# Second attention block: turning x un-normalised, with centred weights, a bias through a diagonal of deviations, and the variance from ScalarE's squares

## The reference

```
def layer_norm(x, gamma, beta):
    mu = jnp.mean(x, axis=-1, keepdims=True)
    var = jnp.mean(jnp.square(x - mu), axis=-1, keepdims=True)
    return (x - mu) * jax.lax.rsqrt(var + LN_EPS) * gamma + beta
q = (decoder_seq @ Wq.T + bq).reshape(B, T_dec, N_HEADS, D_HEAD)
kv = jnp.einsum('bthd,bthe->bhde', k, v)
att = jnp.einsum('bqhd,bhde->bqhe', q, kv) * scale
return layer_norm(att.reshape(B, T_dec, D_MODEL) + decoder_seq, ln_gamma, ln_beta)
...
x = x + jnp.tanh(g_xattn[1]) * _L1_xattn_ref(ctx_1024, _layernorm(x, axis=-1), ...)
x = x + jnp.tanh(g_ffn[1]) * _L1_ffn_ref(_layernorm(x, axis=-1), ...)
```

## Time and profile before

| | us |
|---|---|
| median of 3 runs | 739.65 (737.48 to 742.19) |
| the profiled execution | 736.21 |
| its span, first to last instruction | 734.3 |
| of that: from x back in SBUF (433.07) to the last router norm (484.38) | 51.3 |

### The profile page before, as it was taken

How to read it: one execution, slowest core, us unless ns; L and a number is a source line. 1 busy time by engine, 2 the same in 40 slices (tenths; PEclk the granted TensorE clock), 3 DMA queues, 4 the chain that set the end, 5 groups by cost and what they waited for, 6 DMA issues and landing times.

```text
span 734.3 us, 21433 instructions
## 1 busy us (share of the span) xinstructions
PE 657.8 (90%) x7365; PEld 572.6 (78%) x7366; DVE 482.6 (66%) x1218; ACT 457.4 (62%) x1113; POOL 305.6 (42%) x222
## 2 busy tenths in 40 slices
PE   4777899979988999999999969973999999999993
PEld 4423466758877999988999959862999999999992
DVE  4788678864768866666664468986697545545451
ACT  2465788735568887867766516550898666666651
POOL 1100235434724655554555333331256455554532
PEclk9866699999999999999999998855999999999997
DMA  8980101215559547799876489838564454544451
GB/s 273 371 295 8 29 2 32 85 37 166 145 196 358 85 81 184 187 200 260 215 168 111 65 239 415 289 114 184 122 125 72 73 80 72 85 75 76 70 59 21
DMA packets 114934, 105.08 MB, mean 143 GB/s; under 512 B 53611, under 2 KB 100725, under 8 KB 114246
## 3 DMA queue, kind: packets, MB, share of 16 engines
q1 hardware_dynamic: 99910, 83.93, 38.1%
q0 software_dynamic: 14976, 20.58, 18.6%
HBM read 64.84 MB, written 28.23 MB: 127 GB/s over the span
## 4 chain that ended last, share of the span: by engine, by line
PE 71%; DVE 13%; DMA 4%; ACT 4%; issue 3%; POOL 2%; SPq 1%; POOLq 0%; DVEq 0%; ACTq 0%
PE bank L1217 9%; PE bank L1219 9%; PE bank L1218 9%; PE bank L1230 9%; PE bank L1232 9%; PE bank L1231 9%; PE bank L971 2%; PE bank L972 1%; PE bank L973 1%; DVE ln_stats L2063 1%; DMA x_arena<-token_rows,gather_now 1%; DVE weights L1708 1%; POOL weights L820 1%; PE bank L1112 1%; PE bank L1129 1%
## 5 line engine op out<-in xcount | busy, mean ns | idle before, releaser
L1526 ACT ACTIVATE work<-bank,b_cols 128x128 f32<-128x128 f32 x624 | 178.5, 384 | 135.2 <-PE bank L1219 133.0
L1217 PE MATMUL bank<-x_arena,weights 128*128 128x128 f16 x1248 | 215.3, 220 | 1.3 <-DVE x_arena L1955 1.3
L1218 PE MATMUL bank<-x_arena,weights 128*128 128x128 f16 x1248 | 215.3, 220 | 0.0
L1219 PE MATMUL bank<-x_arena,weights 128*128 128x128 f16 x1248 | 215.3, 220 | 0.0
L1970 DVE TENSOR_TENSOR work<-work 128x512 f16<-128x512 f32 x156 | 101.0, 689 | 113.7 <-ACT work L1534 113.7
L1230 PE MATMUL bank<-weights,work 128*128 x624 | 170.2, 273 | 1.3 <-issue 1.3
L1232 PE MATMUL bank<-weights,work 128*128 x624 | 170.1, 273 | 0.0
L1231 PE MATMUL bank<-weights,work 128*128 x624 | 170.1, 273 | 0.0
L826 POOL DMA_INDIRECT x_arena<-token_rows,gather_now x78 | 81.7, 1047 | 141.8 <-DVE gather_now L1964 105.9
L1217 PEld LDWEIGHTS bank<-x_arena,weights 128*128 x1248 | 122.9, 98 | 2.6 <-DVE x_arena L1955 1.8
L1218 PEld LDWEIGHTS bank<-x_arena,weights 128*128 x1248 | 122.9, 98 | 0.8
(11 more groups left out here) (227 smaller groups left out, 1188.8 us busy)
## 6 DMA issues: line engine op xcount, KB each, us to landing
weights<-in_L_ffn_W SPq DMA_DIRECT2D x76, 256.0 KB, 7.1
raw<-in_L_ffn_W SPq DMA_DIRECT2D x44, 256.0 KB, 4.0
split_dram<-row_arena SPq DMA_DIRECT2D x12, 512.0 KB, 5.5
weights<-split_dram SPq DMA_DIRECT2D x3, 2048.0 KB, 15.9
odd_sum<-padding_row SPq DMA_DIRECT2D x1, 2176.0 KB, 11.5
token_rows<-row_arena SPq DMA_DIRECT2D x1, 2072.0 KB, 10.0
x_arena<-in_x SPq DMA_DIRECT2D x4, 512.0 KB, 6.3
weights<-in_L_ffn_sW SPq DMA_DIRECT2D x8, 256.0 KB, 7.3
```

The lines of the kernel that those rows point to most:

```text
L1217: nc.tensor.matmul(o, w1_at[f][c][0].block(), hi, start=c == 0, stop=False)
L1218: nc.tensor.matmul(o, w1_at[f][c][0].block(), lo, start=False, stop=False)
L1219: m = nc.tensor.matmul(o, w1_at[f][c][1].block(), hi, start=False, stop=c == DC - 1)
L1526: m = nc.scalar.activation(hid[:, k, f * P:f * P + P], h_ps[k][half][:, g * P:g * P + P], ACT.Gelu, bias=b1_cols[n][:, f, bass.ds(e, 1)], ...
```

## The change

x is no longer normalised ahead of the second attention. PE transposes x itself, as soon as the two sums are added. Wq is centred over its inputs, and the folded matrix and the bias over their outputs, so that the means of x and of the result vanish. What the normalisation would have scaled is put on the bias: it is multiplied by the standard deviation of each token, as a matmul with a diagonal matrix (`diag`) that ACT makes from the identity. The second normalisation cancels the common factor; its epsilon is scaled to match (`mid_shift[:, norm1(1, b)]`). The variance of the result is the mean of squares that ACT sums (`accum_out`), so DVE takes no moments of it. The lists of calls on all engines and `MID_NORMS` change with it; `shift1` is left for the router's norms only, so waits on `shift_ready` count to B.

```diff
+diag = work[:, 0:1024].rearrange("p (k t r) -> p k t r", k=2, t=TB)
+squares_out = work[:, 1024:1024 + TB * D].rearrange("p (t d) -> p t d", t=TB)
+kvm_mean = places[:, 0, 0:B * DC].rearrange("p (b c) -> p b c", b=B)
+plus_half = places[:, 1, TT - TB:TT]
+kvb_mean, wq_mean = places[:, 1, 0:B], places[:, 1, B:B + DC]
...
-MID_NORMS = [0, 1, 2, 3, 4, 5, 8, 6, 9, 7, 10, 11]
+MID_NORMS = [0, 1, 2, 4, 8, 3, 5, 9, 6, 10, 7, 11]
...
         pool.wait_ge(var1_ready, after)
-        nc.gpsimd.tensor_tensor(mid_rstd[:, i, :], mid_rstd[:, i, :], minus_half[:, :], ALU.pow).then_inc(rstd1_ready, 1)
+        if i < B:
+            nc.gpsimd.tensor_tensor(mid_shift[:, i, :], mid_rstd[:, i, :], plus_half, ALU.pow).then_inc(rstd1_ready, 1)
+        else:
+            nc.gpsimd.tensor_tensor(mid_rstd[:, i, :], mid_rstd[:, i, :], minus_half[:, :], ALU.pow).then_inc(rstd1_ready, 1)
+    nc.gpsimd.memset(plus_half, 0.5).then_inc(consts_ready, 1)
+    pool.wait_ge(consts_ready, 6)
     for count, i in enumerate(MID_NORMS):
         mid_roots(i, count + 1)
         if count == 9:
             router_rows_low(0)
-    pool.wait_ge(shift_ready, 2 * B)
+    pool.wait_ge(shift_ready, B)
...
     def turned1(b, h):
-        pe.wait_ge(ln_done, 2 * B + half_no(b, h))
+        pe.wait_ge(ln_done, 2 * B + 2 * b + 2)
         if b:
             pe.wait_ge(xlnT_ready, half_no(b - 1, h))
         for c in range(DC):
             for t in range(2):
-                m = nc.tensor.transpose(half_ps(h)[:, c, t * P:t * P + P], normed(8 + b)[:, 2 * h + t, c * P:c * P + P], ident)
+                m = nc.tensor.transpose(half_ps(h)[:, c, t * P:t * P + P], x_sb[:, TB * b + 2 * h + t, c * P:c * P + P], ident)
         m.then_inc(tp_done, 1)
     def attention1(b, h):
+        if h == 0 and b < 2:
+            pe.wait_ge(act_setup, 6 if b == 0 else 10)
+        elif h == 0:
+            pe.wait_ge(attended, TB * (b - 1))
         pe.wait_ge(xlnT_ready, half_no(b, h))
         for t in range(2 * h, 2 * h + 2):
-            i = TB * b + t
             for c in range(DC):
-                m = nc.tensor.matmul(attended_ps(i), xlnT[:, b % 2, c, t * P:t * P + P], kvm[:, b, c, :], start=False, stop=t % 2 == 1 and c == DC - 1)
-            m.then_inc(proj_done, 1)
+                nc.tensor.matmul(attended_ps(TB * b + t), xlnT[:, b % 2, c, t * P:t * P + P], kvm[:, b, c, :], start=t % 2 + c == 0, stop=False)
+    def bias1(b):
+        pe.wait_ge(act_setup, (8, 11, 12, 13)[b])
+        for t in range(TB):
+            nc.tensor.matmul(attended_ps(TB * b + t), diag[:, b % 2, t, :], kvb[:, b, :], start=False, stop=t % 2 == 1).then_inc(proj_done, 1)
...
-    bias1(0)
+    for h in range(2):
+        turned1(0, h)
     for b in range(B):
-        for h in range(2):
-            turned1(b, h)
-        if b == 0:
+        if b == 1:
             folded(2)
             folded_bias(2)
-        else:
-            bias1(b)
+        if b < B - 1:
+            for h in range(2):
+                turned1(b + 1, h)
         for h in range(2):
             attention1(b, h)
+        bias1(b)
...
-        act.wait_ge(pe_setup, 10 + first)
-        for i in range(2):
-            m = nc.scalar.activation(kvm[:, first + i, :, :].rearrange("p c e -> p (c e)"), fold_ps[i][:, :], ACT.Copy)
+        act.wait_ge(dve_setup, 10 + first)
+        for b in range(first, first + 2):
+            for c in range(DC):
+                m = nc.scalar.activation(kvm[:, b, c, :], fold_ps[b - first][:, c * D:c * D + D], ACT.Identity, bias=kvm_mean[:, b, c:c + 1])
         m.then_inc(act_setup, 1)
-        act.wait_ge(pe_setup, 11 + first)
-        nc.scalar.activation(kvb[:, first:first + 2, :].rearrange("p b d -> p (b d)"), kv_ps[first // 2][:, :], ACT.Copy).then_inc(act_setup, 1)
+        act.wait_ge(dve_setup, 11 + first)
+        for b in range(first, first + 2):
+            m = nc.scalar.activation(kvb[:, b, :], kv_ps[first // 2][:, b % 2 * D:b % 2 * D + D], ACT.Identity, bias=kvb_mean[:, b:b + 1])
+        m.then_inc(act_setup, 1)
...
-    def norm_x(b, h):
+    def deviations(b):
+        act.wait_ge(rstd1_ready, rstd1_count(0, b))
         if b >= 2:
-            act.wait_ge(tp_done, B + half_no(b - 2, h))
-        normalise1(x_sb[:, TB * b:TB * b + TB, :], normed(8 + b), norm1(0, b), b + 1, h).then_inc(ln_done, 1)
+            act.wait_ge(proj_done, TT + TB * (b - 1))
+        for t in range(TB):
+            m = nc.scalar.activation(diag[:, b % 2, t, :], ident, ACT.Copy, scale=mid_shift[:, b, t:t + 1])
+        m.then_inc(act_setup, 1)
+    def attended_squares(b, h):
+        act.wait_ge(proj_done, TT + TB * b + 2 * h + 2)
+        if b:
+            act.wait_ge(squared, half_no(b - 1, h))
+        for t in range(2 * h, 2 * h + 2):
+            m = nc.scalar.activation(squares_out[:, t, :], attended_ps(TB * b + t), ACT.Square, accum_out=mid_mv[:, norm1(1, b), t, 1:2])
+        m.then_inc(squared, 1)
...
-    halves(norm_x, 0)
     halves(read_out1, 0)
+    deviations(0)
+    halves(read_out1, 1)
     folded_out(2)
-    halves(norm_x, 1)
-    halves(read_out1, 1)
-    halves(norm_x, 2)
-    halves(norm_x, 3)
+    deviations(1)
+    halves(attended_squares, 0)
     halves(read_out1, 2)
+    deviations(2)
+    halves(attended_squares, 1)
     halves(read_out1, 3)
+    deviations(3)
     for b in range(B):
+        if b + 2 < B:
+            halves(attended_squares, b + 2)
...
+        link(V.reduce_sum(wq_mean, late_wq, AX))
+        link(V.tensor_scalar(wq_mean, wq_mean, 1.0 / D, None, ALU.mult))
+        for e in range(DC):
+            V.tensor_scalar(late_wq[:, e, :], late_wq[:, e, :], wq_mean[:, e:e + 1], None, ALU.subtract)
...
+    def folded_means(first):
+        dve.wait_ge(pe_setup, 10 + first)
+        for i in range(2):
+            m = V.reduce_sum(kvm_mean[:, first + i, :], fold_ps[i][:, :].rearrange("p (c e) -> p c e", c=DC), AX)
+        link(m)
+        V.tensor_scalar(kvm_mean[:, first:first + 2, :], kvm_mean[:, first:first + 2, :], -1.0 / D, None, ALU.mult).then_inc(dve_setup, 1)
+        dve.wait_ge(pe_setup, 11 + first)
+        link(V.reduce_sum(kvb_mean[:, first:first + 2], kv_ps[first // 2][:, :].rearrange("p (b e) -> p b e", b=2), AX))
+        V.tensor_scalar(kvb_mean[:, first:first + 2], kvb_mean[:, first:first + 2], -1.0 / D, None, ALU.mult).then_inc(dve_setup, 1)
...
+    def merge(b):
+        dve.wait_ge(x_back[b], 32)
+        V.tensor_tensor(batch(b), batch(b), odd_rows[b], ALU.add).then_inc(ln_done, 2)
     def x_statistics(b):
-        dve.wait_ge(x_back[b], 32)
-        link(V.tensor_tensor(batch(b), batch(b), odd_rows[b], ALU.add))
+        dve.wait_ge(ln_done, 2 * B + 2 * b + 2)
         statistics1(lambda t: x_sb[:, TB * b + t, :], 0)
+        variance1(0, b)
+        dve.wait_ge(var1_ready, MID_NORMS.index(norm1(0, b)) + 1)
+        V.tensor_scalar(mid_shift[:, norm1(1, b), :], mid_rstd[:, norm1(0, b), :], EPS, None, ALU.mult)
     def add_beta(b):
-        dve.wait_ge(ln_done, 2 * B + 2 * b + 2)
+        dve.wait_ge(tp_done, B + half_no(b, 1))
         V.tensor_tensor(batch(b), batch(b), beta.unsqueeze(1).broadcast_to([P, TB, D]), ALU.add).then_inc(beta_ready, 1)
-    def attended_moments(b):
-        statistics1(lambda t: attended_ps(TB * b + t), TT + TB * b)
-        variance1(1, b)
     def scale_attended(b):
         i = norm1(1, b)
-        for t in range(TB):
-            V.scalar_tensor_tensor(scaled[:, b % 2, t, :], attended_ps(TB * b + t), mid_mv[:, i, t, 0:1], gamma, ALU.subtract, ALU.mult)\
-             .then_inc(attended, 1)
+        for h in range(2):
+            dve.wait_ge(squared, half_no(b, h))
+            V.tensor_tensor(scaled[:, b % 2, 2 * h:2 * h + 2, :], attended_bank(b, h), gamma.unsqueeze(1).broadcast_to([P, 2, D]), ALU.mult).then_inc(attended, 2)
+        V.scalar_tensor_tensor(mid_rstd[:, i, :], mid_mv[:, i, :, 1], 1.0 / D, mid_shift[:, i, :], ALU.mult, ALU.add).then_inc(var1_ready, 1)
...
+    folded_means(0)
+    merge(0)
     x_statistics(0)
-    variance1(0, 0)
-    for b in range(1, B):
-        x_statistics(b)
-        shift1(0, b - 1)
-        variance1(0, b)
+    merge(1)
+    x_statistics(1)
+    merge(2)
+    folded_means(2)
+    x_statistics(2)
     add_beta(0)
-    shift1(0, 3)
-    add_beta(1)
-    attended_moments(0)
     scale_attended(0)
-    add_beta(2)
-    attended_moments(1)
+    merge(3)
     add_attention1(0)
     router_moments(0)
+    x_statistics(3)
+    add_beta(1)
     scale_attended(1)
-    add_beta(3)
-    shift1(2, 0)
-    attended_moments(2)
+    shift1(0)
+    add_beta(2)
     add_attention1(1)
     router_moments(1)
     scale_attended(2)
-    shift1(2, 1)
-    attended_moments(3)
+    shift1(1)
+    add_beta(3)
     add_attention1(2)
     router_moments(2)
     scale_attended(3)
-    shift1(2, 2)
+    shift1(2)
     add_attention1(3)
     router_moments(3)
-    shift1(2, 3)
+    shift1(3)
```

(13 more changed lines are left out.)

13 lines of the change are left out of this document (7 added, 6 removed).

## The result

The changed kernel takes 745.16 us in the median of 17 runs (742.68 to 749.05), the kernel before beside it 739.5 us (736.55 to 742.19, 17 runs): a ratio of 1.0082, interval 1.0065 to 1.0099, so it is slower by 4.8 to 7.3 us. The forecast was 746.8 us in 741.0 to 750.0. The profiled execution of the changed kernel took 746.54 us, with a span of 744.7 us.

What follows compares the result with a forecast made beforehand. DVE was taken to bound the second half of the middle. Its work shrinks by 3.8 us, but waits put `last_norm` at 491.6 instead of 484.4, 7.2 us late: 739.65 + 7.2 = 746.8 us, range 741.0 to 750.0.

Steps and rivals of the forecast that it cites:

- The wait for the second fold: DVE stands before `folded_means(2)` until PE's second fold, moved behind batch 0's attention and bias, ends at 451.1: 8.4 us.
- Rival one: PE keeps 2.4 GHz through the first attention, so the fold ends 2.8 earlier: +4.4, 744.1 us; chance 0.22.
- The start: On DVE `folded_means(0)` stands ahead of the first sum, which ends at 436.0, 1.7 us later than before.
- The squares: ACT's squares out of PSUM, in no row: taken as 0.49 us; half a batch is there at 457.3 for scaling.
- Rival two: ACT is dearer, or PE falls to 1.2 GHz in its gap (466 to 469): +1.4, 748.2 us; chance 0.15.
- The roots: POOL's root of the variance meets DVE's sum or beta and ends 0.9 us after it, delaying the addition.
- Rival four: POOL's root goes first and keeps DVE's sum out; `merge(1)` and transposes 0.9 late: +8.1, 747.8 us; chance 0.10.
- Batch 3: POOL takes root 10 and `router_rows_low(0)` before root 7, so DVE idles 2.7 us before the last addition.
- Rival three: The wait for the second fold costs nothing: -1.2, 738.4 us; with POOL's roots hidden too, 733.9; chance 0.08.

Runs made afterwards that it cites:

- the early fold: Changed kernel with PE making the second fold and its bias right behind the first 8 transposes, instead of behind batch 0's attention and bias: 737.64 us, ratio 0.9974.
- the experiment: Changed kernel with `router_rows_low(0)` on POOL moved behind root 6 and the last addition of batch 2, to run beside DVE's moments: 743.39 us, ratio 1.0062.
- the three reorders: Changed kernel with PE's second fold early, DVE's variance ahead of both scalings, and POOL's `router_rows_low(0)` beside DVE's moments: 734.61 us, ratio 0.9939.

## Why the prediction held

- **The wait for the second fold.** Forecast 8.4 us, measured 8.30, and 7.07 to 8.52 in the five profiles with this order: the mechanism is right, and that it fits to 0.1 us is luck. The working gave 2.8 us of it to the low clock; the runs give 1.4 to 2.9. Rival one (PE keeps 2.4 GHz) did not come about.
- **The start.** The first sum was to end 1.7 us later than before. Counted from the first key product it is 3.3 later in the profile, of which 1.6 is the first fold's clock and the rest the forecast. The new reductions of 512 elements, in no row of before, took 0.69 against the estimate of 0.69; centring Wq cost nothing, since the masked products (L1737) start 3.78 us behind the first key product, against 3.76 before. DVE's busy time fell by 0.84 us although it now contains the centring (1.5 us, which the forecast did not count) and the 1.9 us in which a variance instruction is held; without these the work is 4.2 us less, by the forecast 3.8.
- **The squares.** One takes 0.36 to 0.43 us, with a row of its own behind it for reading the sum; they follow each other 0.35 apart, not 0.49. It changed nothing, as DVE's scaling waits only 0.25 us for them. Rival two's first half (ACT dearer) falls: it is the other way round, as the moments on DVE cost 5 us. Of its second half the low clock is there, but it costs nothing: batch 1's attention takes 5.41 us instead of 3.62 behind a gap of 2.15, and the squares behind it are done 4 us before DVE scales. The logits of batch 2 take 3.50 us, as before (3.49; those of batch 0 take 1.95), and end at 495.7, while `last_norm` ends only at 499.6.
- **The roots.** Forecast 0.9 us on the path for each of batches 0 to 2, measured 0.96, 0.97 and 0.96. Rival four, the root ahead of the sum keeping DVE out, did not come about: the root of 445.59 took 1.01 us and the sum of 445.62 its usual 1.24. The root of 442.26, which started behind the sum of 442.22, took 2.10.
- **Batch 3: nearly the right sum, half the mechanism wrong.** The step said that root 7 would come 2.7 us late "because POOL's order tells", with root 10 and `router_rows_low(0)` ahead of it, so that DVE would be idle 2.7 us before the last addition. There are 1.11 us idle and, ahead of them, 1.87 us by which the variance instruction itself is too long (2.02 instead of 0.15): 3.0 us in all. POOL's order is only half of it: with the order changed DVE lost the same time in its additions. What was missing is that DVE and this POOL instruction shut each other out. The rule of the Trainium skill (SBUF — State Buffer, section Who interferes with whom) says just this of a VectorE instruction with two SBUF inputs and a GpSimd instruction that reads SBUF, and the trace agrees here, 2.02 and 3.40 us for instructions of 0.15 and 1.67. The prediction had set it aside because a root beside additions cost nothing; that observation also stands, so the rule holds for the long instruction and, with DVE as the loser, not visibly for the short one.
- **Rival three, the other side.** It priced the kernel without the wait at 738.4 us and without the roots' waits as well at 733.9. The change alone did not get there, but the reorders did: 737.64 with the early fold, 734.61 with all three.
- **The total.** The terms gave 7.2 us and the profile shows 6.9 without the slower first fold; the medians give 5.7, the ratio 4.8 to 7.3. That 6.9 comes so close is luck in part: the wait alone differs by 1.5 us between profiles.

## What to carry to other kernels

A change that takes work off the bounding engine can still lose if it makes that engine wait in line for a product that nobody on it waited for before: here the consumer moved from ACT to DVE, and what was by the prediction's count 3.8 us less work on DVE became 6.9 us more time. Whoever adds such a wait should move the producer in the same change; one reorder on PE gave all of it back, and with two more the changed kernel is ahead of the one before by 0.6%. A short result that another engine must turn around (a variance and its root) should be issued ahead of the long work that can run beside it, and a long POOL instruction over SBUF should be laid beside DVE's moments, not beside its instructions with two SBUF inputs. Beside `last_norm`, which has one, it is not free either, as told below.

## What the hardware showed that was not expected

- A POOL instruction of 2.06 us (`router_rows_low`, 128x1024) held a DVE instruction of 128x4 for 2.02 us instead of 0.15, and four additions for 3.40 instead of 1.67. DVE's moments (BATCH_NORM_STATS2, x4) beside the same instruction took 1.41 us, as everywhere; the POOL instruction took 2.06 there in the experiment, and 2.27 in the profile of before, where the last addition (until 475.67) still ran as it began (475.32). A scaling with one input in SBUF and one in PSUM also kept its time beside it: 1.29 us from 493.82, beside POOL's 493.03 to 495.09, in the kernel with the moments on DVE.
- An instruction with a single tensor in SBUF as input can be as slow beside it, and neither kernel avoids that: `last_norm`, two TENSOR_SCALAR of 128x256 with one tensor and two columns as inputs, takes 4.32 us beside POOL's two pieces (495.31, 4.13 us), 4.33 in the profile before. The same form in the first layer (L1774) takes 0.46 us each in the mean of 32. With DVE's next instruction right behind it (499.51), that is some 3.4 us of DVE's time in every version here; no run moved POOL's pieces away from it, so the cause is argued from the rows alone, and what moving them would return is open. A TENSOR_SCALAR of 128x4 that met the end of POOL's piece (480.41, in the kernel with the piece beside moments) took 0.28 instead of 0.17.
- Between a root on POOL (128x4) and a 1024-element sum or beta on DVE it matters who starts first. Where the sum or beta did, by 0.04 to 0.25 us, the root took 1.9 to 2.1 us instead of 1.01, and DVE kept its 1.21 to 1.23. Where the root did, by 0.03 us, neither lost more than the trace resolves (1.01, and 1.24 for DVE). Beside a scaling out of PSUM the root takes 1.01.
- A square with a sum on ACT shows two rows, ACTIVATE with 0.40 us and a read of the accumulator with 0.23, which overlap with the next; the pitch is 0.35 us. The timeline of ACT in the changed kernel:

```profile
460.01 0.40 ACT L1593 ACTIVATE work<-bank 128x256 f32<-128x256 f32 x1
460.27 0.23 ACT L1593 ACTIVATION_READ_ACCUMULATOR work<-bank 128x1 f32 x1
460.36 0.41 ACT L1593 ACTIVATE work<-bank 128x256 f32<-128x256 f32 x1
```

- The clock of the same work differs from one execution to the next: no experiment changes PE's first fold, and the window of 430 to 435 us had 0.69 in the changed kernel's profile, 0.74 and 0.66 in two of the experiments', and 1.00 in that of the three reorders, whose first key product starts at the same time (427.29); the price is 1.6 us.
